# Second attention: VectorE's steps split into single operations and reordered between chains

## What is computed

```
xn = layernorm(context, g, b);  ln = layernorm(layernorm(x), g, b)
q = ln @ Wq.T;  k, v = concat([xn @ Wkv.T, ln @ Wlkv.T])       # 4 heads of 64
attn = softmax(mask(rmsnorm(q) * 64**-0.5 @ rmsnorm(k).T))
x = x + tanh(g_xattn[1]) * (attn @ v @ Wo.T + bo)
s = sigmoid(layernorm(x) @ Wg.T)                               # 16 experts in 4 groups
keep the 2 groups with the largest maximum, in them the 4 best experts
w = 2.5 * s / sum(s of the 4)
```

## Time and profile before

| what | value |
|---|---|
| median of 3 runs | 2014.36 us (2007.49 to 2015.08) |
| the profiled execution's own time | 2014.43 us |
| its span, first to last instruction | 2012.7 us |
| mean granted clock of TensorE | 0.961 of full speed |
| busy over the span | PE 91%, PEld 69%, DVE 71%, ACT 54%, POOL 55% |
| the second attention | from about 1026 us to about 1654 us |

### The profile page before, as it was taken

How to read it: one execution, slowest core, us unless ns; L and a number is a source line. 1 busy time by engine, 2 the same in 40 slices (tenths; PEclk the granted TensorE clock), 3 DMA queues, 4 the chain that set the end, 5 groups by cost and what they waited for, 6 DMA issues and landing times. The chain is left out here.

```text
span 2012.7 us, 42245 instructions
## 1 busy us (share of the span) xinstructions
PE 1829.3 (91%) x12013; PEld 1397.4 (69%) x12013; DVE 1421.6 (71%) x4429; ACT 1086.1 (54%) x2699; POOL 1108.1 (55%) x1278
## 2 busy tenths in 40 slices
PE   5999999999999489999959999999999829999997
PEld 4888888888888368888836666666666516777775
DVE  4788888888887632233247999999999746666665
ACT  2545545555544423333348888888888724444443
POOL 2444444454544245445555788888888643555555
PEclk9999999999999589999979999999999859999999
DMA  4121111111115223333321111111111954655654
GB/s 138 42 64 37 39 31 42 29 42 28 42 29 211 72 43 50 52 54 53 50 48 30 53 49 56 54 58 56 49 56 54 325 168 83 102 94 92 99 96 65
DMA packets 138661, 142.52 MB, mean 71 GB/s; under 512 B 31835, under 2 KB 128835, under 8 KB 138057
## 3 DMA queue, kind: packets, MB, share of 16 engines
q1 hardware_dynamic: 98826, 93.03, 15.6%
q0 software_dynamic: 37888, 44.51, 13.7%
q10 hardware_dynamic: 1726, 2.28, 0.4%
HBM read 90.01 MB, written 51.94 MB: 71 GB/s over the span
## 5 line engine op out<-in xcount | busy, mean ns | idle before, releaser
L2010 POOL DMA_INDIRECT out<-y,xr x115 | 178.3, 1550 | 174.4 <-DVE y L2048 95.6
L938 POOL TENSOR_SCALAR prob<-prob,rc 100x363 f32<-100x363 f32 x256 | 147.4, 586 | 177.7 <-DVE rc L752 174.8
L647 ACT ACTIVATE prob<-psS,nm 100x361 f32<-100x361 f32 x256 | 141.7, 563 | 79.2 <-DVE nm L747 79.2
L1662 POOL DMA_INDIRECT rows<-row,pos_of x128 | 141.0, 1102 | 52.1 <-issue 31.2
L1746 POOL DMA_INDIRECT acc<-y,slots x57 | 90.4, 1585 | 136.8 <-DVE y L1804 124.0
L1781 DVE TENSOR_TENSOR hid<-psU,gate 128x512 f32<-128x512 f32 x57 | 39.4, 692 | 159.0 <-PE psU L1898 159.0
L1643 POOL TENSOR_TENSOR rk<-rk,neghalf 121x12 f32<-121x12 f32 x64 | 130.0, 2030 | 5.3
L2092 ACT ACTIVATE x_hi<-psX 128x128 fp32r<-128x128 f32 x115 | 31.9, 278 | 185.4 <-PE psX L2123 177.0
L747 DVE TENSOR_REDUCE nm<-psS 100x2 f32<-100x722 f32 x128 | 116.0, 906 | 17.2 <-PE psS L536 9.4
L2032 DVE TENSOR_TENSOR pre<-psG,late 128x512 f32<-128x512 f32 x115 | 79.5, 691 | 68.2 <-PE psG L2136 67.7
L2152 PE MATMUL psD<-expert_w,hT 128*128 x460 | 120.3, 384 | 1.2 <-ACT hT L2103 1.2
(11 more groups left out here) (346 smaller groups left out, 5809.3 us busy)
## 6 DMA issues: line engine op xcount, KB each, us to landing
xr<-rows SPq DMA_DIRECT2D x115, 136.5 KB
expert_w<-in_L_ffn_moe_w SPq DMA_DIRECT2D x8, 1024.0 KB
late<-in_ctx SPq DMA_DIRECT2D x32, 181.5 KB
cT<-in_ctxT SPq DMA_DIRECT2D x32, 180.5 KB
cT<-in_ctxT SPq DMA_DIRECT2D x64, 90.2 KB
expert_w<-in_L_ffn_moe_w SPq DMA_DIRECT2D x8, 512.0 KB
expert_w<-in_L_ffn_W1T SPq DMA_DIRECT2D x16, 256.0 KB
expert_w<-in_L_ffn_W3T SPq DMA_DIRECT2D x16, 256.0 KB
```

Source lines behind the costliest of these rows:

```text
L647: s.activation(prob[:, q, 0:S], psS[0:N, h, 0:S], ACT.Exp, bias=nm[:, q:q + 1], accum_out=rs[:, q:q + 1]).then_inc(exp_done, 1)
L938: g.tensor_scalar(prob[:, q, :], prob[:, q, :], rc[:, q:q + 1], 1.0, ALU.mult, ALU.mult).then_inc(prob_done, 1)
L1662: g.indirect_dma_start(rows, bass.IndirectOffsetOnAxis(pos[:, b % 4, k:k + 1], 0), row[:, b % 4, :], None).then_inc(slots_out[b % 2], 16)
L2010: g.indirect_dma_start(acc, bass.IndirectOffsetOnAxis(row_token[:, j % RING, :], 0), y[:, j % 4, :], None, compute_op=ALU.add).then_inc(sc ...
```

## The change

Nothing is computed differently. VectorE's composite steps are cut into steps of one operation each (`maxes` becomes four `head_max` and two `shifts`; `y_add` becomes `y_add`, `y_stats`, `y_means`; the four router steps become 24 steps; `ctx_norm`, `ctx_stats` and `ctx_low` are called once for each chunk), and the list of VectorE is written anew so that most operations of one chain stand between operations of others. The lists of TensorE, ScalarE and GpSimd are reordered too, and with TensorE's the order in which the two banks of `psJ` are used. Four waits are written out that the old order implied: `head_max` waits for the transpose of the batch before (`t_mm`), `one_plus` for the last weights, `experts_chosen` for the last `y_rank`, and `slots` for the last positions. VectorE's loop has one more turn. SyncE's list is as it was.

The diff, cut (the router steps left out are one operation each, as `group_max`):

```diff
-PROJECTIONS = ((2, "lt"), (2, "ct1"), (2, "kv0"), (1, "qt"), (1, "kt0"), (2, "q"), (1, "kt1"), (2, "kv1"), (2, "kv3"), (2, "kv2"), (3, "ct0"))
+PROJECTIONS = ((2, "ct1"), (1, "qt"), (2, "kv0"), (1, "kt0"), (2, "q"), (2, "kv1"), (1, "kt1"), (2, "kv3"), (2, "kv2"), (3, "ct0"), (3, "lt"))
...
         for i in range(-3, B + 1):
-            at(i - 1, p_transpose, 1)
-            at(i, scores, 1)
-            at(i + 2, lat_transpose)
             at(i + 2, ctx_transpose, 1)
             at(i - 1, values, 1)
             at(i - 1, y_out)
+            at(i + 1, q_transpose)
             at(i + 2, qkv, 1)
             at(i, p_transpose, 0)
-            at(i + 1, q_transpose)
             at(i + 1, k_transpose, 0)
             at(i - 1, y_transpose)
             at(i + 2, qkv, 0)
             at(i - 1, y_logits)
+            at(i + 2, qkv, 2)
             at(i + 1, k_transpose, 1)
-            at(i + 2, qkv, 2)
             at(i + 1, scores, 0)
             at(i + 2, qkv, 4)
             at(i + 2, qkv, 3)
+            at(i, values, 0)
+            at(i, p_transpose, 1)
             at(i - 1, y_rank)
-            at(i, values, 0)
             at(i + 3, ctx_transpose, 0)
+            at(i + 1, scores, 1)
+            at(i + 3, lat_transpose)
         t.wait_ge(plan, PLANNED)
...
         for i in range(-3, B + 1):
-            at(i, exps, 0)
             at(i - 1, values, 1)
             at(i + 2, lat_transposed)
             at(i + 2, ctx_transposed, 1)
             at(i, normalise, 0)
+            at(i + 1, q_transposed)
             at(i + 2, ctx_high)
             at(i + 2, qkv, 1)
-            at(i + 1, q_transposed)
+            at(i - 1, y_transposed)
             at(i + 1, k_transposed, 0)
-            at(i - 1, y_transposed)
             at(i + 2, qkv, 0)
             at(i - 1, sigmoid_exp)
             at(i, exps, 1)
+            at(i + 2, qkv, 2)
+            at(i, p_transposed, 0)
             at(i + 1, k_transposed, 1)
-            at(i, p_transposed, 0)
-            at(i + 2, qkv, 2)
             at(i + 2, square, 0, 3, "kv1", ssA, sqA)
             at(i, normalise, 1)
             at(i + 2, qkv, 4)
             at(i + 2, qkv, 3)
             at(i, values, 0)
             at(i + 2, square, 3, 5, "kv2", ssB, sqB)
+            at(i, p_transposed, 1)
             at(i + 3, ctx_transposed, 0)
-            at(i, p_transposed, 1)
+            at(i + 1, exps, 0)
...
-        def maxes(b, p):
-            if p == 0:
+        def head_max(b, hh):
+            if hh == 0:
                 v.wait_ge(mask_done, b + 1)
-            for h in range(2):
-                hh = 2 * p + h
-                v.wait_ge(s_mm, H1 * b + hh + 1)
-                v.tensor_tensor_reduce(prob[:, hh, :], psS[0:N, h, 0:K1], mb[:, b % 2, :], 1.0, -3e38,
-                                       ALU.add, ALU.max, nm[:, hh:hh + 1]).then_inc(add_done, 1)
+            if b >= 1:
+                v.wait_ge(t_mm, pairs * (b - 1) + hh // 2 + 1)
+            v.wait_ge(s_mm, H1 * b + hh + 1)
+            v.tensor_tensor_reduce(prob[:, hh, :], psS[0:N, hh % 2, 0:K1], mb[:, b % 2, :], 1.0, -3e38,
+                                   ALU.add, ALU.max, nm[:, hh:hh + 1]).then_inc(add_done, 1)
+
+        def shifts(b, p):
             v.wait_ge(add_done, H1 * b + 2 * p + 2)
             v.wait_ge(rkA, 2 * b + 2)
             v.scalar_tensor_tensor(nm[:, 2 * p:2 * p + 2], nm[:, 2 * p:2 * p + 2], -1.0, rk[0:N, b % 3, 0, 2 * p:2 * p + 2],
...
+        def y_stats(b):
             v.wait_ge(x1_done, b + 1)
-            v.bn_stats(r["st1"][:, :], x1[:, par, :]).then_inc(ln1_dve, 1)
+            v.bn_stats(r["st1"][:, :], r["x1"][:, b % 2, :]).then_inc(ln1_dve, 1)
+
+        def y_means(b):
             v.wait_ge(ln1_dve, nth(LN, b, "stat"))
             v.bn_aggr(r["mv1"][:, :], r["st1"][:, :]).then_inc(ln1_dve, 1)
...
+        def group_max(b):
+            v.wait_ge(route, nth(ROUTE1, b, "s1"))
+            v.tensor_reduce(gmax[:, 0:GROUPS], grouped, AX, ALU.max).then_inc(route, 1)
+
+        def group_top(b):
+            v.wait_ge(route, nth(ROUTE1, b, "gm"))
+            v.max(gtop[:, :], gmax[:, :]).then_inc(route, 1)
...
+        def experts_chosen(b):
+            v.wait_ge(route, nth(ROUTE1, b, "hot"))
+            if b >= 1:
+                v.wait_ge(rk_mm, b)
+            v.tensor_reduce(chosen[:, :], hot[:, :, :].rearrange("p k e -> p e k"), AX, ALU.add).then_inc(route, 1)
+
+        def weight_sum(b):
+            v.wait_ge(route, nth(ROUTE1, b, "cho"))
+            v.tensor_reduce(tmp[:, 0:1], top_v[:, 0:TOP1], AX, ALU.add).then_inc(route, 1)
...
+        def slots(b):
             v.wait_ge(rk_mm, b + 1)
+            if b >= 1:
+                v.wait_ge(dispatch, nth(DISPATCH, b - 1, "posi"))
             v.tensor_tensor(r["slot_of"][:, :], psY[0:N, 0:E1], base[0:N], ALU.add)
-            n = dp.inc(v.tensor_scalar(row[:, b % 4, D:D + 1].bitcast(I32), c["token"][:, :], 0.0, None, ALU.add))
-            v.wait_ge(dispatch, n)
-            v.tensor_scalar(c["token"][:, :], c["token"][:, :], float(N), None, ALU.add)
-            n = dp.inc(v.tensor_tensor(base, psY[:, 2 * E1:3 * E1], base, ALU.add))
-            v.wait_ge(dispatch, n)
-            n = dp.inc(v.tensor_tensor(r["hit"][:, :, :], r["hot"][:, :, :],
-                                       r["slot_of"][:, :].unsqueeze(1).to_broadcast([N, TOP1, E1]), ALU.mult))
-            v.wait_ge(dispatch, n)
-            n = dp.inc(v.tensor_reduce(r["pos_f"][:, :], r["hit"][:, :, :], AX, ALU.add))
-            v.wait_ge(dispatch, n)
-            dp.inc(v.tensor_copy(pos[:, b % 4, :], r["pos_f"][:, :]))
+            v.tensor_scalar(row[:, b % 4, D:D + 1].bitcast(I32), token[:, :], 0.0, None, ALU.add).then_inc(dispatch, 1)
+
+        def advance(b):
+            v.wait_ge(dispatch, nth(DISPATCH, b, "slot"))
+            v.tensor_scalar(token[:, :], token[:, :], float(N), None, ALU.add)
+            v.tensor_tensor(base, psY[:, 2 * E1:3 * E1], base, ALU.add).then_inc(dispatch, 1)
...
-        for i in range(-4, B + 1):
-            at(i + 3, ctx_norm)
+        for i in range(-4, B + 2):
+            at(i - 1, sigmoid)
+            at(i - 1, group_max)
+            at(i - 1, group_top)
+            at(i + 3, ctx_norm, 0)
+            at(i - 2, places)
+            at(i - 1, group_index)
+            at(i + 3, ctx_norm, 1)
+            at(i - 1, group_float)
+            at(i - 1, group_hot)
+            at(i + 1, head_max, 0)
+            at(i - 1, group_ok)
             at(i, reciprocals, 1)
-            at(i - 1, route_top)
+            at(i - 1, group_shift)
+            at(i - 1, masked)
+            at(i + 3, x_norm)
+            at(i - 1, expert_top)
             at(i + 2, sum_squares, 0, 3, sqA, ssA)
-            at(i + 1, maxes, 0)
-            at(i - 1, y_dispatch)
-            at(i + 3, x_norm)
+            at(i - 1, expert_index)
+            at(i - 1, expert_float)
+            at(i - 1, expert_hot)
+            at(i + 1, head_max, 1)
+            at(i - 1, experts_chosen)
+            at(i + 3, ctx_norm, 2)
+            at(i + 4, x_stats)
+            at(i + 4, ctx_stats, 0)
             at(i + 2, sum_squares, 3, 5, sqB, ssB)
-            at(i + 1, maxes, 1)
+            at(i + 1, shifts, 0)
+            at(i + 4, ctx_stats, 1)
+            at(i + 2, rms_scale, 1, 3, rkA, knA)
+            at(i + 1, head_max, 2)
+            at(i + 4, x_means)
+            at(i - 1, slots)
+            at(i - 1, weight_sum)
+            at(i + 4, ctx_stats, 2)
+            at(i - 1, advance)
+            at(i - 1, weight_scale)
             at(i + 1, reciprocals, 0)
-            at(i + 4, ctx_stats)
+            at(i - 1, hits)
+            at(i - 1, weights)
+            at(i + 4, ctx_means)
+            at(i + 1, head_max, 3)
             at(i, y_add)
-            at(i + 2, rms_scale, 1, 3, rkA, knA)
+            at(i + 1, shifts, 1)
+            at(i, y_stats)
+            at(i - 1, weights_scaled)
+            at(i, y_means)
+            at(i - 1, positions)
             at(i + 2, rms_scale, 3, 5, rkB, knB)
             at(i, y_norm)
-            at(i - 1, route_weights)
-            at(i + 3, ctx_low)
-            at(i + 4, x_stats)
-            at(i, route_groups)
+            at(i + 3, ctx_low, 0)
+            at(i + 3, ctx_low, 1)
+            at(i, one_plus)
...
         for i in range(-3, B + 4):
-            at(i + 1, rms, 3, 5, ssB, rkB)
-            at(i - 3, scatter, 0)
             at(i - 1, y_norm)
+            at(i + 2, ctx_mid)
             at(i + 3, ctx_norm)
-            at(i + 2, ctx_mid)
+            at(i + 2, mask)
+            at(i + 3, x_norm)
             at(i - 3, scatter, 1)
-            at(i + 3, x_norm)
-            at(i + 2, mask)
+            at(i - 3, scatter, 2)
+            at(i + 2, rms, 0, 3, ssA, rkA)
+            at(i - 4, scatter, 3)
+            at(i + 2, rms, 3, 5, ssB, rkB)
+            at(i - 2, scatter, 0)
             at(i + 1, add_bias)
-            at(i - 3, scatter, 2)
```

(62 more changed lines are left out.)

86 lines of the change are left out of this document (29 added, 57 removed).

## The result

The median rose from 2014.57 us to 2033.53 us (four runs each, 2007.49 to 2015.08 and 2029.57 to 2037.04). The ratio is 1.0104 [1.0086, 1.0123]: slower by 1%. The forecast was 2006 us, from 1988 to 2027.

What follows compares the result with a forecast made beforehand. VectorE's bound of 17.92 us a turn was to give way to a loop over GpSimd of 17.1 plus 0.3, 17.4; 26 turns save 13.5 us, the end costs 5, so 2006 us from 2014.43, range 1988 to 2027.

Steps and rivals of the forecast that it cites:

- VectorE's own turn: VectorE's queue without waits: splitting 19 adjacent dependent pairs at 0.11 us each takes it from 17.44 to 15.3 us.
- The last rival: On VectorE the small operations' gap is the semaphore's, so no overlap: turn 17.7 to 18.4, 2014 to 2030 us; chance 0.08.
- The ring: Loop from GpSimd's rms A and scatters through VectorE's y_norm, TensorE's scores and back to sum_squares A: 17.1 us a turn.
- its idle time: Sign on GpSimd: before one scatter in four, 0.5 us or so over the usual 0.21, ended by a DMA.
- The landing hidden: Rival on GpSimd: rms B covers scatter 3's landing, loop 16.6 plus 0.3, 1990 us; chance 0.31.
- G: On GpSimd, time from the end of one scatter's issue to the next issue that waits for its landing; taken as 2.8 us.
- the estimate on which that rival leaned: Skill's DMA rule for GpSimd's scatter of 109 KB: landing 2.25 us from the issue, under 1.2 after its end.
- `values` and `oT`: On TensorE, y_rank behind values 0 ends the 0.6 wait for chosen; the oT wait of 0.36 stays, floor 16.7 us.
- ScalarE closes no loop: The path y_transposed, exps 1, square A in ScalarE's queue was left out as shorter; a loop there would fail the prediction.
- the lock that the prediction set aside: VectorE and GpSimd share an SBUF port pair exclusively; add_bias would wait for a whole rms_scale, turn 17.6 or 17.7 us.
- The last turns: End of the stage, where expert weight loads slow landings: 4.0 us once, 0 to 4 the next turn; 5 us charged.
- The rival of the late landing: On GpSimd scatter 0 waits behind scatter 3 with G at 3.91: turn 18.5, 2035 us; chance 0.15.

Runs made afterwards that it cites:

- e7: Changed kernel with six multiplications whose result nobody reads ahead of y_transpose, filling TensorE's wait; 2027.62 us, ratio 1.0073 to the kernel before.
- e1: Changed kernel with scatter 3 put back ahead of rms A in GpSimd's list; 1990.28 us, ratio 0.9896 to the kernel before.
- e14: Changed kernel with VectorE's rms_scale B moved ahead of y_add, away from add_bias; 2011.7 us, ratio 0.9998 to the kernel before.
- e2: Changed kernel with ctx_mid put behind ctx_norm in GpSimd's list, no longer beside y_norm; 2030.56 us, ratio 1.0105 to the kernel before.
- e9: Kernel before the change with one swap: scatter 3 behind rms A in GpSimd's list; 2035.0 us, ratio 1.0114 to the kernel before.
- e8: As e1, with mask put between the root and ctx_mid in GpSimd's list; 1989.78 us, ratio 0.9885 to the kernel before.
- e3: Changed kernel with add_bias put ahead of scatter 0 in GpSimd's list, while the landing is awaited; 1993.43 us, ratio 0.9901 to the kernel before.

## Why the prediction was wrong

**VectorE's own turn (right).** 19 dependences at 0.11 made 15.3; it is 15.1. Small independent operations start 0.05 to 0.1 apart. The last rival, that the overlap is not had, is out.

**The bound moves to the loop over GpSimd (right).** The ring that the prediction adds up is the ring of waits after. The waits for `chosen` went, the root wait is over 1 us, `head_max` 0 waits for `psS`, each scatter 0 has its idle time of 0.58, which is 0.35 or so over the usual 0.21 to 0.24 and not 0.5, and is not booked to a DMA. The landing hidden (G of 2.3 or less) did not hold: from the start of the issue of `scatter` 3 to the `scatter` 0 that it frees 3.7 us pass (1414.74 to 1418.48), well over the estimate on which that rival leaned. `values` and `oT` are as foreseen, and ScalarE closes no loop: VectorE is through with the router's steps that wait for it at 1408.91 (1408.74 + 0.17), and still waits 0.34 for `psS`.

**The size of the loop (wrong).** Step by step in the turn shown, in us:

| step | forecast | measured |
|---|---|---|
| `rms` A to its end | 2.86 | 1414.50 - 1411.69 = 2.81 |
| `scatter` 3 | 1.29 | 1.32 |
| G | 2.8 | 2.66 |
| `scatter` 0 | 1.0 | 1.09 |
| `add_bias` | 0.82 | 1.40 |
| root | 0.95 | 1403.91 - 1402.93 = 0.98 |
| `y_norm` to `y_transpose` | 0.47 | 1404.88 - 1403.91 = 0.97 |
| to `qkv` 2 | 1.39 | 1406.27 - 1404.88 = 1.39 |
| to `head_max` 0 | 3.1 | 1409.25 - 1406.27 = 2.98 |
| to the end of `sum_squares` A | 2.38 | 1411.69 - 1409.25 = 2.44 |
| sum | 17.1 | 18.0 |

Eight of ten terms are within 0.15. The other two are collisions of VectorE and GpSimd: `add_bias` with `rms_scale` B, +0.58, for which I had put 0.3, and `y_norm` with `ctx_mid`, +0.50, which I had not seen. What it needs was at hand, in the new list of GpSimd: `ctx_mid` stands right behind the root, whose end is the very event that `y_norm` waits for, so the two meet in every turn (`y_norm` takes 0.92 in all of them from 1110 to 1540 us). The turn came out at 18.05, not 17.4. Over the 26 turns this is 23 x 0.65 = 15 us of the 26.5 that separate 26 x 17.4 = 452.4 from 478.94. The Trainium skill (SBUF — State Buffer, "SBUF: two separate sides") has the lock that the prediction set aside as giving 17.6 or 17.7. For `add_bias` the trace agrees in size, 0.62 lost to an operation of 0.68, though by the records `add_bias` starts first, by 0.10. And the Trainium skill (SBUF — State Buffer, "Who interferes with whom") names `tensor_scalar` among the operations that can take the shared pair, which is `y_norm`'s form. The 0.92 against 0.41 agrees in direction only: `ctx_mid` runs for 0.77 more after `y_norm` starts (1403.91 to 1404.68), and 0.51 is lost.

**TensorE's clock (not in the prediction).** Six turns are 119.94 - 6 x 18.05 = 11.6 us over the usual one, and each holds a drop of the granted clock to 1.2 GHz; no such drop lies in the 26 turns of the kernel before. The longest, 21.71, also has a late landing, G = 1251.82 - 1248.17 = 3.65:

```profile
1251.82 1.43 POOL L1749 DMA_INDIRECT rows<-row,pos_of  x1 [1.56 <-DVE pos_f L1595]
```

The row names `pos_f`, but in the usual turn that is written after `scatter` 0 has started (1401.57 against 1400.45), so the wait is not for it; the landing is what is left. In `e7` such a landing costs 0.7 of a turn; by that, an estimate, some 11 of the 11.6 us go with the clock. What TensorE did before the drop at 1218: it waited 1.54 us for `row`, where the earlier trace rows have 0.18. It waits so in the turns without a drop too (1.60 at 1404.88), so the wait alone does not call one. In the drop `qkv` 2's first product takes 0.76, in the usual turn 0.47. `e1`, with a wait of 0.6, has no drop in its 26 turns, nor has `e7`, where the wait is filled. But with about 1.1 a turn `e14` has none and `e2` has two, and of the two turns of `e9` with a wait of 1.62 one has a drop. So the drops go with a slow loop and long waits, and which turn gets one stays open. Usual turn and drops together make the 26.5.

**The last turns (mis-sized).** I charged 5 us; it was 59.94 - 51.06 = 8.9. The GpSimd rows show G at 6.0 (1581.89 to 1587.89) and 6.77 (1605.22 to 1611.99), as the earlier trace rows had it (6.76), but in two turns in full, where I had let the second cost 1 us, and the two turns take 22.7 and 22.3 us. The DMA queues move 355 and 341 GB/s in these two waits (1581 to 1588 and 1605 to 1612 us), and 53 over the steady turns. `e9` shows the same 8.5 from the swap alone, and of the kernels of the table every one with `scatter` 3 behind `rms` A has an end of 55.6 to 60.3, every one with it ahead 47.3 to 51.1.

**The sum.** 26.5 us from the turns and 3.9 from the end, less 5.1 by which `y_add` of batch 2 came earlier and 0.7 behind the stage, lead from 2006 to 2030.6. The 5.1 is no effect to count on: the first `y_add` stands anywhere from 1070.1 to 1077.8 us in the profiles of the table's kernels. The rival of the late landing named 2035 with G at 3.91; the time was near to it, its mechanism was not there: G was 2.66. Its place was right, the queue behind `scatter` 3; its price came from elsewhere.

**What stays open.** `e1` and `e8` meet at 17.07, where GpSimd's queue is all but full; TensorE waits 0.6 a turn for `row` and 0.35 for `oT` in `e1` and is busy for the rest. No run separates the two. `e3`, at 16.97, has 1.1 us a turn of idle time on GpSimd, so its turn is set by something else. `e1` still has the collision of `y_norm` with `ctx_mid`. Nothing here tells why some landings of the steady turns come late, nor why the usual turn of `e9` is 18.18 and not 18.7.

## What to carry to other kernels

When an edit turns an engine's queue into slack, walk the ring of waits that is left, and in it ask of each step what now runs beside it on the engine that shares its way to memory: two operations released by one event met in every turn here. And look whether an engine's own queue is full before shortening a step of another. An instruction that waits for a DMA's landing needs the longest work of its queue between the two, sized for the stretch where transfers are slowest and not for the steady one. Freed slack on the matrix engine is not free either: waits of 1.1 to 2.3 us went with drops of its clock here.
